# The larger factor of a routing table: GpSimd differences and ScalarE squares for VectorE comparisons, with the table's products placed in other slots

## What is computed

```python
xn = layernorm(x)
x  = x + attention(xn) + experts(xn)

# attention: RWKV-6, heads of 64 channels, per head and step t
y_t[i] = sum_j r_t[j] * (S[i,j] + u[j]*k_t[j]*v_t[i])
S[i,j] = S[i,j]*exp(w_t[j]) + k_t[j]*v_t[i]

# experts: one of 8 for each token
expert = argmax(softmax(tokens @ Wr + br))
h = relu(token @ W1[expert] + b1[expert])
out = (h @ W2[expert] + b2[expert]) * max_prob
```

## Time and profile before

| | us |
|---|---|
| median of 3 runs | 646.92 |
| lowest, highest run | 644.90, 649.61 |
| the profiled execution | 645.12 |
| its span | 643.8 |

### The profile page before, as it was taken

The page is one execution under the profiler, slowest core; times in us unless marked ns, Lnnn a source line. Parts: engine busy times, 40 slices in busy tenths (PEclk is TensorE's granted clock), DMA queues, the critical chain, the costliest instruction groups (busy, mean ns, idle before and its releaser), DMA issues.

```text
span 643.8 us, 19310 instructions
## 1 busy us (share of the span) xinstructions
PE 573.7 (89%) x7666; PEld 490.5 (76%) x7666; DVE 440.9 (68%) x1094; ACT 280.6 (44%) x596; POOL 193.5 (30%) x147
## 2 busy tenths in 40 slices
PE   2799365987899999999999999999999999999795
PEld 1789353975789898989888779898778888787583
DVE  5685578687867767676768685858585768685422
ACT  3576110133354545545453436353446363535341
POOL 4120011003134333342524232333323343323323
PEclk9889685998999999999999999999999999999988
DMA  9998790695133324243342415142414243221322
GB/s 283 221 286 224 196 259 1 227 315 107 25 68 60 75 49 85 44 85 50 62 73 45 79 25 92 35 86 43 83 26 92 42 87 48 32 37 32 61 35 33
DMA packets 60762, 61.31 MB, mean 95 GB/s; under 512 B 5137, under 2 KB 55058, under 8 KB 60530
## 3 DMA queue, kind: packets, MB, share of 16 engines
q1 hardware_dynamic: 47858, 45.27, 27.1%
q0 software_dynamic: 11840, 14.42, 14.9%
q10 hardware_dynamic: 976, 0.38, 0.2%
HBM read 41.32 MB, written 23.07 MB: 100 GB/s over the span
## 4 chain that ended last, share of the span: by engine, by line
PE 74%; DVE 11%; SPq 5%; issue 4%; DMA 3%; POOL 1%; ACT 0%; DVEq 0%; ACTq 0%; POOLq 0%
PE F L571 11%; PE F L563 10%; PE LL L451 7%; PE G L383 7%; PE YB L540 4%; PE G L352 4%; PE G L399 4%; PE YB L496 4%; PE YB L494 2%; PE YB L521 2%; PE YB L525 2%; SPq L1562 2%; PE G L414 2%; DVE mix L886 2%; PE YB L313 2%
## 5 line engine op out<-in xcount | busy, mean ns | idle before, releaser
L1443 POOL DMA_INDIRECT out<-ys,dst_row x39 | 65.5, 1679 | 205.5 <-DVE ys L1002 193.2
L886 DVE SCALAR_TENSOR_TENSOR mix<-G,vec,ba 128x256 f32<-128x256 f32 x160 | 69.6, 477 | 15.9 <-PE G L352 15.3
L922 DVE COPY_PREDICATED AP_<-msk,LL 128x256 f32<-128x256 uint32 x96 | 51.1, 532 | 41.3 <-PE LL L451 39.2
L563 PEld LDWEIGHTS F<-xsT,w1s 128*128 128x128 f32 x624 | 73.7, 192 | 7.3 <-issue 5.4
L571 PE MATMUL F<-w,hsT 128*128 x312 | 78.0, 394 | 0.8 <-ACT hsT L1294 0.8
L563 PE MATMUL F<-xsT,w1s 128*128 128x128 f32 x624 | 78.1, 278 | 0.7 <-ACT xsT L1276 0.7
L1294 ACT ACTIVATE hsT<-F,b1c 128x128 f32<-128x128 f32 x156 | 44.6, 368 | 67.4 <-PE F L563 67.4
L451 PEld LDWEIGHTS LL<-R,K 64*64 64x64 f32 x2560 | 46.6, 138 | 28.9 <-issue 20.9
L938 DVE TENSOR_TENSOR R<-R,D 128x256 f32<-128x256 f32 x112 | 50.1, 447 | 25.7 <-issue 19.0
L451 PE MATMUL LL<-R,K 64*64 64x32 f32 x2560 | 55.1, 225 | 13.3 <-DVE D L940 13.3
L571 PEld LDWEIGHTS F<-w,hsT 128*128 128x128 f32 x312 | 58.2, 193 | 10.1 <-issue 1.4
(11 more groups left out here) (151 smaller groups left out, 1096.0 us busy)
## 6 DMA issues: line engine op xcount, KB each, us to landing
cd<-cd_d SPq DMA_DIRECT2D x32, 320.0 KB, 6.1
w<-in_W SPq DMA_DIRECT2D x16, 512.0 KB, 8.7
cd_d<-cd SPq DMA_DIRECT2D x32, 160.0 KB, 3.4
b2t<-in_b SPq DMA_DIRECT2D x39, 128.0 KB
w<-in_x SPq DMA_DIRECT2D x8, 512.0 KB, 9.7
xn_d<-w SPq DMA_DIRECT2D x8, 512.0 KB
out<-in_x SPq DMA_DIRECT2D x8, 512.0 KB, 8.9
out<-res POOLq DMA_DIRECT2D x16, 256.0 KB, 4.4
```

The lines of the kernel that those rows point to most:

```text
L563: i1 = pe.matmul(FB[:, k * P:(k + 1) * P], w1s[:, cc, k, :], xsT[:, cc, :], start=(cc == 0), stop=(cc == 1))
L886: i1 = dve.scalar_tensor_tensor(mixed_in(u, c, n, cc), bk[:, cc * UN:(cc + 1) * UN], cvec(LAM + CC * n, cc), ba[:, cc, :, :].rearrange("p ...
L922: dve.copy_predicated(to, m, now.rearrange("p g (n t) -> p g n t", t=B)).then_inc(s["a"])
L1443: pool.indirect_dma_start(io["out"], bass.IndirectOffsetOnAxis(dst_row[:, f:f + 1], 0), ys[:, f % 2, :], None, compute_op=ALU.add).then_in ...
```

## The change

`at_row` is no longer compared on VectorE. GpSimd writes the difference of the row number n and the token's row into `at_row`, in four instructions of 128x1024 behind L1493. ScalarE squares it in place and then takes relu(1 - square), which is 1 where the difference is 0 and else 0, again in place: eight instructions of 128x1024. Two of the four groups stand ahead of ScalarE's `decay(1, 0)` and two behind it. TensorE's products of the table are moved: `table(0)` to ahead of level 5, `table(1)` ahead of level 6, `table(2)` behind it, and `table(3)` behind `receptance(1, 0)`.

```diff
 # TensorE
             key(1, 0)
             mixed(1, 0, 3)
+            table(0)
             level(0, 0, 5)
             value(1, 0)
             mixed(1, 0, 4)
-            table(0)
+            table(1)
             level(0, 0, 6)
+            table(2)
             receptance(1, 0)
-            for g in range(1, 4):
-                table(g)
+            table(3)
             block(0, 0)
 # VectorE
-            def at_rows(g):
-                iota = rout[:, IOTA:IOTA + P].rearrange("p (o n) -> p o n", o=1).broadcast_to([P, 8, P])
-                dve.tensor_tensor(at_row[:, 8 * g:8 * g + 8, :], iota, bcast(placef[:, 1, 8 * g:8 * g + 8], P), ALU.is_equal).then_inc(s["ohp"])
...
             levels(0, 0, 2)
-            at_rows(0)
             mixed(1, 0, 1)
             added(1, 0, 1)
             levels(0, 0, 3)
-            at_rows(1)
             mixed(1, 0, 2)
             added(1, 0, 2)
             levels(0, 0, 4)
-            at_rows(2)
             experts_of_tiles()
             key(1, 0)
             mixed(1, 0, 3)
             added(1, 0, 3)
             levels(0, 0, 5)
-            at_rows(3)
             mixed(1, 0, 4)
 # ScalarE
+            def at_rows(g):
+
+                act.wait_ge(s["dis"], g + 1)
+                a = at_row[:, 8 * g:8 * g + 8, :].rearrange("p t n -> p (t n)")
+                act.activation(a, a, ACT.Square).then_inc(s["sqd"])
+                act.wait_ge(s["sqd"], g + 1)
+                act.activation(a, a, ACT.Relu, scale=-1.0, bias=con[:, ONE:ONE + 1]).then_inc(s["ohp"])
...
             decay_down(1, 0)
+            at_rows(0)
+            at_rows(1)
             decay(1, 0)
+            at_rows(2)
+            at_rows(3)
             value(1, 0)
 # GpSimd
             pool.tensor_tensor(to, to, bcast(rout[:, ROW:ROW + NT], FT), ALU.mult).then_inc(s["att"])
+
+            iota = rout[:, IOTA:IOTA + P].rearrange("p (o n) -> p o n", o=1).broadcast_to([P, 8, P])
+            for g in range(4):
+                pool.tensor_tensor(at_row[:, 8 * g:8 * g + 8, :], iota, bcast(placef[:, 1, 8 * g:8 * g + 8], P), ALU.subtract).then_inc(s["dis"])
             difference(0, 1)
```

More of the change, by code:

```diff
@@ L170, in program @@
             "ls bst wvc ew1 ew2 "
-            "step exp cnt slot att ohp inv back srow drow ex "
+            "step exp cnt slot att dis sqd ohp inv back srow drow ex "
             "cr0 cr1 "
```

## The result

The changed kernel takes 651.67 us in the median of 14 runs (649.05 to 653.66), the kernel before 647.48 in 14 (644.61 to 649.61). The ratio is 1.0066, with a 95% interval of 1.0051 to 1.0082: +4.3 us, 3.3 to 5.3. The forecast was +3.0 us, 649.6, with 645.5 to 653.5 as its range.

What follows compares the result with a forecast made beforehand. VectorE was taken to bound the stretch up to the second unit's key matmuls, TensorE behind. Holding 5.6 less comparisons 2.3 gave +3.3 to +3.4; 3.4 - 0.4 = +3.0 us, 646.6 + 3.0 = 649.6, range 645.5 to 653.5.

Steps and rivals of the forecast that it cites:

- The place: From 95 us: VectorE bounds up to the second unit's key matmuls at 112.63, TensorE behind them; later VectorE effects are hidden.
- The holding: From 100.04 us: GpSimd's four differences hold off VectorE's two-input SBUF instructions 1.78 us each, 7.1 in all, net loss 5.6.
- the replay: VectorE's order stepped through from 100.04 us with a GpSimd turn at each two-input wait; level 2 ends at 108.9, not 103.31.
- the rival that needed 2.65 us an instruction: GpSimd's differences, with two broadcast inputs, run longer than 1.78 us; from 2.65 each, slower beyond 1%; chance 0.04.
- longer holding: Rival: GpSimd keeps the inputs through all four differences without giving a turn, +4.5 us; only L886 held too, +3.8; chance 0.17.
- What the comparisons give: Ahead of the key matmuls: two L844 comparisons of 1.14 us gone from VectorE, gain 2.3, key +3.3 to +3.4 us late.
- The third comparison: The L844 in front of VectorE's key product, which waits for the key matmuls (end 115.33) anyway; taken at nothing.
- The order of products: TensorE between level 5 and the value's matmuls: the moved table(0) fills a gap, -0.4 us.
- ScalarE: Its eight instructions, about 1.07 us each, are hidden around decay(1, 0) and delay neither copies nor table products; taken at nothing.
- The clock: Rival: TensorE's full clock comes one table product and one projection later, both taking twice their time; +6.6 us, 653.2; chance 0.07.
- if the full clock came later: Sign, to be read in the changed kernel's trace, that the forecast would be wrong: TensorE regains its full clock later.
- The total: Whole kernel: net 3.4 - 0.4 = +3.0 us, let through to the end, 649.6; the forecast case +1.5 to +4, chance 0.56.

Runs made afterwards that it cites:

- diffs_only: Kernel before plus GpSimd's four differences, written to a spare part of w2 nobody reads, VectorE still making its comparisons; ratio 1.0077 to before.
- writes_only: Kernel before plus eight GpSimd memsets of 128x1024 to a spare part of w2; ratio 0.9997 to before.
- order_only: Kernel before with nothing changed but the slots of TensorE's table products; ratio 0.9996 to before.
- scalar_only: Kernel before plus eight ScalarE instructions of 128x1024 in the places of the change, on a spare part of w2; ratio 1.0008 to before.
- dummies_last: Kernel before plus 16 dummy matmuls behind TensorE's last instruction, where nobody waits for them; ratio 0.9958 to before.
- scalar_alone: Changed kernel without GpSimd's differences: ScalarE makes the squares itself in 32 instructions of 128x128, and the four relus; ratio 0.9975 to before.
- warm: Changed kernel plus ten dummy matmuls of 128x128 in the stretch where TensorE waits for VectorE; ratio 1.0007 to before.
- scalar_warm: ScalarE's squares without GpSimd's differences, plus 16 dummy matmuls where TensorE waits for VectorE; ratio 0.9887 to before.
- before_warm: Kernel before plus 16 dummy matmuls where TensorE waits for VectorE between 92 and 111 us; ratio 0.9945 to before.

## Why the prediction was right

- *The place.* Right: VectorE's part up to the key matmuls and TensorE's behind it. In the changed kernel the chain runs without a gap from the key to the block.
- *The holding.* Right in kind and close in size. Forecast were turns of 1.78 us from VectorE's end to GpSimd's; the first difference has 1.76 (100.61 to 102.37). What L937 loses by it is 1.70 (2.04 on the chain less its own 0.34), since it ends 0.28 behind GpSimd, as L939 did in the kernel before, where the replay added a whole 0.34 each time. Forecast was a loss of 5.6 us at the end of level 2; the four instructions are 5.3 too long. diffs_only has it alone at 5.4, and writes_only, that a GpSimd which only writes holds nothing. The rate from two rows of other lengths was good to 1%, two broadcast inputs cost nothing extra (the rival that needed 2.65 us an instruction is out), and GpSimd gave VectorE a turn after each difference (longer holding is out as well). L883 passes, by its 0.86 us.
- *What the comparisons give.* 2.28 us, right: the key starts 3.10 us late where +3.3 to +3.4 was forecast.
- *The third comparison.* Taken at nothing because VectorE's key product "in any case waits for the key matmuls (end 115.33)". The chain of the kernel before reads otherwise: the product waited for the third L844 and the three small steps behind it, and began 0.38 us after those matmuls' end.

```profile
113.64 1.14 DVE w L844
...
115.71 0.69 DVE K L902
...
116.53 1.97 PE G L399 x8
```

  So the gap ahead of the value's matmuls was this comparison's doing, and by these rows dropping it would close the gap without moving a product, which was not tried. The sum isn't wrong by it, since the gap is counted once, under the order of products.
- *The order of products.* -0.4 forecast, -0.55 measured in order_only.
- *ScalarE.* At nothing, right; scalar_only.
- *The clock.* This step failed, and with it came one of the prediction's own signs of being wrong, "if the full clock came later". It was weighed as a rival with 0.07, because "the sequence just ahead of the key is the same". It is, and the full clock came later all the same: 3.64 us for the key instead of 2.70, and 0.69 instead of 0.59 for the mixture behind it. One profile for each kernel could mislead, but the seven with VectorE's chain up to the key as before lie at 2.59 to 2.78, and the three with its holds and no dummies at 3.33 to 3.64. The distance from the key's start to L464 is 16.10 us in the changed kernel and 15.06 in order_only with the same work, so the clock took 1.04 us. The rival was priced at 3.6 us in all for two pieces at half speed; under a third came. Against the sum: 3.10 - 0.55 + 1.04 = +3.59, the measured distance, where 3.4 - 0.4 = 3.0 was forecast. The sum comes that near partly by luck: the holding and the order were 0.3 and 0.15 us better than forecast and took back 0.45 of the clock's 1.04.
- *The total.* 3.6 us in the stretch, 3.85 at the next L464, 4.3 (3.3 to 5.3) timed. Whether the rest is real or is the kind of shift that dummies_last shows can't be said from these runs. The interval holds 3.6, begins just above the forecast's 3.0 and also holds the +4.5 of *Longer holding*, so the time alone doesn't tell these two apart; the durations of VectorE's four instructions do. The forecast time of 649.6 is 2.1 us below the measured 651.67: 1.2 by the change, and 0.9 because the kernel before came out at 647.48, not 646.6.

What stays open is what raises the clock, and with it why the change made it rise later. TensorE's wait ahead of level 2 is 1.30 us before and 3.00 after, but scalar_alone has 1.30 as well and still takes 3.01 for the key matmuls. The dummies raised it in warm and in scalar_warm and not in before_warm, where TensorE was busy for 8.19 us of the 10 from 100 to 110 and the clock stayed at 0.50.

## What to carry to other kernels

Before giving VectorE's work to GpSimd, look in the trace for a VectorE instruction with two SBUF inputs under a GpSimd one that reads: its excess is the price, and the work moved costs the bound engine more (1.70 us for 1024 elements, less what overlaps) than the comparison did itself (1.14). ScalarE's squares held nothing here (the key starts at 17.27 in scalar_alone, the 2.26 us of the comparisons earlier than before); 32 small squares with a bias were the better way. When a few us are at stake, measure the distance between two instructions that all versions have, behind everything that was moved, and give a version with more instructions a control with as many that nobody waits for.

## What the runs showed of the hardware beside that

- TensorE's clock is worth most of what the change costs in the stretch (3.6 us): ten dummy matmuls took 2.85 us out of it, 1.18 ahead of the key and 1.67 in it.
- The time ahead of the comparison, in which the inputs are loaded, ranged from 89.1 to 94.3 us between profiles of kernels that are nearly alike there, and was 93.1 and 92.5 in two profiles of the same kernel.
